# Decoder layer on one core: products of exponentials and values, four heads at a time in place of two

## The chip, the core and the metric

The kernel runs on one core of a Trainium2 chip. The metric is the device time of one execution in microseconds (us). Five engines work side by side: TensorE (PE, with its weight loads as PEld), VectorE (DVE), ScalarE (ACT), GpSimd (POOL) and SyncE (SP), which here issues all transfers.

## The reference

The layer takes x (32 sequences of 64 rows, 256 wide) and a context of the same shape. Each of three steps is followed by a residual sum and a normalization: causal self-attention with 16 heads of 16; a cross-attention with rotary positions; a two-matrix feed-forward part with quantized weights. The change touches the cross-attention only. It treats the 64 rows of a sequence as 64 channels (8 heads of 8 channels) and the 256 columns as positions:

```python
q = _apply_rotary(q_emb, split_heads(_proj(x, Wq, bq)))   # 8 heads, 256 positions, 8 channels
k = _apply_rotary(k_emb, split_heads(_proj(c, Wk, bk)))
v = split_heads(_proj(c, Wv, bv))
scores = jnp.einsum('bhtc,bhsc->bhts', q, k) / math.sqrt(K_CH)
p_attn = jax.nn.softmax(scores, axis=-1)
out = jnp.einsum('bhts,bhsc->bhtc', p_attn, v)
```

## The kernel before

**Tiling.** The 32 sequences are 16 pairs; a pair fills 128 partitions. The order of every engine's work is written out by hand. Phase A does both attentions for all pairs in a software pipeline of 16 bodies, one per pair `i`; most are in a hardware loop (`Fori`). Two more phases do the feed-forward part and aren't touched.

**A body has 16 slots.** In body i, slot s, TensorE does:

- `max_tile` (L541): scores of two heads, for the row maxima, 14 tiles ahead. From slot 2 on these are tiles of pair i+1.
- `exp_tile` (L561): the same scores, transposed and with the negated maximum added through two extra rows of `QA`, into bank `e_b[s % 2]`.
- one piece of other work of the pipeline, if the slot has one (below).
- `pv_tile` of the tile before, s - 1 (L576): exponentials times values.

ScalarE turns each `e_b` bank into exponentials, 128x512, in `PB[:, n % 4]` (L731), so four tiles fit. VectorE reduces each max tile (L912).

**pv_tile.** Tile n holds two heads and 128 of the 256 key positions. For each head one matmul contracts over the 128 positions: 32 stationary columns (8 channels, and ones whose product is the sum of the exponentials, up to the 32 of a column group) and 256 moving columns, float32, into PSUM partitions 32j to 32j+31. j is `2 * hp + e`, hence a tile uses two of the four 32-wide column groups; the next tile, with `hp = 1`, uses the other two. A float32 matmul shows as two records in the trace.

**Other work in the slots**, with j = i+2 and a = i+3: slot 0 `qk_proj(a)` (L454); 1 `u_transpose` (L226); 2 `max_transpose(i, 1)` (L549); 3 `transpose_p(j)` (L485); 4 `self_pv(j)` (L498: 16 matmuls of 32 stationary and 64 moving columns, float32, over the four column groups); 5 `out_proj(j)` (L507) and `att_transpose` (L233); 6 `rotary_proj("k", j)`; 7 `x_out_proj`; 8 `rotary_proj("q", j)`; 9 `xv_proj`; 11 `v_proj(a)`; 12 `u_transpose` and `max_transpose(i+1, 0)`; 13 and 14 `scores(a)` (L469, L473). Slots 10 and 15 have none.

**From a projection to the scores of a pair.** This is the longest detour of the pipeline. After `out_proj(j)` in slot 5, VectorE takes the statistics of the first normalization (L873 to L878), POOL the root (L292, L294), VectorE normalizes (L885) and rotates k and q (L893). POOL splits k and then q into three bfloat16 parts (`split_parts`, L835 to L845, five operations each). SP stores the parts of k in HBM (L331), issues the loads that spread them over `KA` (L345), stores the parts of q (L331), stores the row maxima (`max_rows`, L359, from `MR` into two rows of `QA`), moves `VM` (L354), waits until the parts of q have landed, and issues the three loads of `QA` (L345). SP does all this in this order. The next body's slot 2 begins with the max tile that reads this `QA` (pair j = i+2 of body i is the next pair of body i+1). The exp tile of slot 0 waits for the row maxima from `max_rows`.

Of the kernel before, what the change touches and what calls it, by code (L numbers as in the profile page):

```python
# [27 lines left out]
NPAIR = 16  # L28
# [42 lines left out]
def build_layer(nc, x, xT, ctx, wpT, woT, xW, xB, rows, w1T, w2T, attn_tables, rotary_tables, out):  # L71
    with ExitStack() as outer:
# [11 lines left out]
        def event(name, steps=1):  # L84
            return Event(sem(name), steps)
# [108 lines left out]
        mrow = [[sem(f"mrow{p}{b}") for b in range(2)] for p in range(2)]  # L194
        mx_ps, mx_red, negm = event("mx_ps", 16), event("mx_red", 16), event("negm", 4)
        mt_ps, mt_sb = event("mt_ps", 2), event("mt_sb", 2)
        e_ps, e_sb, pv = event("e_ps", 16), event("e_sb", 16), event("pv", 16)
        s_wabs, s_wtot, s_wq = sem("s_wabs"), sem("s_wtot"), sem("s_wq")
        s_wround, s_wclip = sem("s_wround"), [sem(f"s_wclip{k}") for k in range(2)]
        NEXPAND = 16 * 3  # L200
# [3 lines left out]
        def wait(eng, ev, pair, step):  # L204
            eng.wait_ge(ev.sem, ev.at(pair, step))  # L205
# [233 lines left out]
        def _(pe):  # L439
# [123 lines left out]
                                            QA[0:K_EXP, 2 * i.p + b, h, :], start=True, stop=True)  # L563
                last.then_inc(e_ps.sem, 1)

            def pv_tile(i, n):

                b, (s4, sc, hp) = n // 8, ((n // 4) % 2, (n // 2) % 2, n % 2)
                if n % 8 == 0:
                    wait(pe, xv_sb, i, 1)  # L570
                    if has(i, 1):
                        wait(pe, u_sb, i.plus(-1), b + 1)
                wait(pe, e_sb, i, n + 1)
                for e in range(2):
                    j = 2 * hp + e
                    last = nc.tensor.matmul(u_b[b][32 * j:32 * j + 32, D * s4:D * s4 + D],  # L576
                                            VA[:, i.p, sc, b, 4 * s4 + j, :], PB[:, n % 4, e, :],
                                            start=sc == 0, stop=sc == 1)
                last.then_inc(pv.sem, 1)

# [40 lines left out]
            def body(i, first=False, selfs=True, rotary=True, last=False):  # L621
# [9 lines left out]
                for s in range(16):  # L631
                    nxt, n = tile_at(i, s + AHEAD)
                    if not last or s + AHEAD < 16:
                        max_tile(nxt, n)
                    exp_tile(i, s)
                    if s == 0 and not first:
                        pv_tile(prev, 15)
                    if s == 0 and selfs:
                        qk_proj(a)
                    if s == 1 and not first:  # L640
                        u_transpose(pe, prev, 1, use(g_b[1], u_nrm, prev, 4))
                    if s == 2:
                        max_transpose(i, 1, 0)
                    if s == 3 and rotary:
                        transpose_p(j)
                    if s == 4 and rotary:
                        self_pv(j)
                    if s == 5 and rotary:
                        out_proj(j)
                    if s == 5 and not first:  # L650
                        att_transpose(pe, prev, use(g_b[1], at_sb, prev, 1))
                    if s == 7 and not first:
                        x_out_proj(pe, prev, use(g_b[0], ln2, prev, 1))
                    if s == 8 and rotary:
                        rotary_proj("q", g_b[1], j)
                    if s == 6 and rotary:
                        rotary_proj("k", g_b[1], j)
                    if s == 9 and not last:
                        xv_proj(i.plus(1))
                    if s == 11 and selfs:  # L660
                        v_proj(a)
                    if s == 12:
                        u_transpose(pe, i, 0, use(g_b[0], u_nrm, i, 2))
                        if not last:
                            max_transpose(i.plus(1), 0, 1)
                    if s == 13 and selfs:
                        scores(a, (0,))
                    if s == 13 and isinstance(i.v, int) and i.v == 13:
                        weight_total(1)
                    if s == 14 and selfs:  # L670
                        scores(a, (1,))
                    if s:
                        pv_tile(i, s - 1)

            bodies(pe, body)
            pv_tile(Pair(0, NPAIR - 1), 15)


        @block.scalar
        def _(act):  # L680
# [46 lines left out]
            def exp_tile(i, n):  # L727
                wait(act, e_ps, i, n + 1)
                if has(i, 1) or n >= 4:
                    act.wait_ge(pv.sem, 16 * i.v + n - 3)  # L730
                nc.scalar.activation(PB[:, n % 4].rearrange("p e t -> p (e t)"), e_b[n % 2][:, :], ACT.Exp,  # L731
                                     scale=XC ** -0.5).then_inc(e_sb.sem, 1)

            def u_copy(i, b):
                wait(act, pv, i, 8 * b + 8)
                if b == 1:
                    wait(act, ut_ps, i, 1)
                elif has(i, 1):
                    wait(act, ut_ps, i.plus(-1), 2)
                nc.scalar.activation(US[:].rearrange("p s t -> p (s t)"), u_b[b][:, :], ACT.Copy).then_inc(u_sb.sem, 1)  # L740
# [108 lines left out]
        def _(dve):  # L849
# [47 lines left out]
            def xv_bias(v):  # L897
                wait(dve, xv_ps, v, 1)
                if has(v, 2):
                    wait(dve, pv, v.plus(-2), 16)  # L900
                dst = VA[:, v.p].rearrange("p s b h c -> p (s b) h c")[:, :, :, 0:XC]
                nc.vector.tensor_tensor(
                    dst, g_b[0][:, 0:D].rearrange("p (q h c) -> p q h c", q=4, h=XH),
# [549 lines left out]
```

## Time and profile before

| | |
|---|---|
| time, median of 3 runs | 742.56 us (738.97 to 747.3) |
| span of the profiled execution | 750.5 us |
| PE busy | 583.4 us, 78% |
| DVE busy | 532.3 us, 71% |
| ACT busy | 387.6 us, 52% |
| POOL busy | 314.5 us, 42% |
| exponentials times values (L576) | 165.7 us busy, 1024 records |

The profiled execution's own time is its span; no other time of it is given. Phase A takes the first 570 us of it, the two feed-forward phases the rest. Busy time counts the union of the records of an engine, so matmuls that run side by side in different column groups count once. "Idle before" is how long an engine stood still ahead of an instruction, with what ended that. PEclk is TensorE's granted clock, 1.00 being 2.4 GHz and 0.50 being 1.2 GHz; a value between is a stretch with both.

### The profile page before, as it was taken

Reading aid. Unit: us, or ns where it says so; the run is one execution under the profiler, and the core shown is the slowest. Engines: PE = TensorE matmul, PEld = TensorE weight load, DVE = VectorE, ACT = ScalarE, POOL = GpSimd, SP = SyncE. Lnnn points to the kernel's source line nnn. Section 1 sums busy time; section 2 is a strip of 40 time slices with the busy share of each in tenths; the row PEclk is TensorE's granted clock in tenths of the full one; section 3 lists DMA queues with packets and bytes.
Section 4 is the critical chain, followed back from the end, with each engine's and each line's share of the span. In section 5 each row is a group of like instructions: output and inputs, shape, how many; then the busy total and the mean of one; then the engine's idle time right before and its main releaser. Section 6 shows DMA issues by size and latency. Waiting matters only on the chain. (4 is left out here: it accounts for less than half of the span.)

```text
span 750.5 us, 13775 instructions
## 1 busy us (share of the span) xinstructions
PE 583.4 (78%) x4002; PEld 319.4 (43%) x4002; DVE 532.3 (71%) x1081; ACT 387.6 (52%) x682; POOL 314.5 (42%) x382
## 2 busy tenths in 40 slices
PE   4656798998989989899998989988697632555455
PEld 3441445454554545445454454534242211333333
DVE  5468376867768777686877878757463767888886
ACT  3220344544545445444555444546565886777764
POOL 3432344443424544244452444514002006776764
PEclk9676699999999999999999999989897885555555
DMA  7112411212121121211212112121100000000000
GB/s 224 48 33 57 152 37 54 65 37 65 42 58 40 52 69 32 68 41 53 64 36 68 44 52 61 35 56 36 34 2 0 1 0 0 14 14 21 14 22 29
DMA packets 60044, 34.37 MB, mean 46 GB/s; under 512 B 20976, under 2 KB 59248, under 8 KB 59888
## 3 DMA queue, kind: packets, MB, share of 16 engines
q1 hardware_dynamic: 60016, 34.03, 15.3%
q8 instruction: 13, 0.21, 0.1%
q14 instruction: 15, 0.12, 0.1%
HBM read 24.32 MB, written 8.39 MB: 44 GB/s over the span
## 5 line engine op out<-in xcount | busy, mean ns | idle before, releaser
L731 ACT ACTIVATE PB<-e_b 128x512 f32<-128x512 f32 x256 | 152.5, 597 | 207.5 <-PE e_b L561 205.6
L912 DVE TENSOR_REDUCE MX<-mx_b 128x2 f32<-128x512 f32 x256 | 174.2, 686 | 100.2 <-PE mx_b L541 97.3
L576 PE MATMUL u_b<-PB,VA 128*32 128x256 f32 x1024 | 165.7, 403 | 0.8 <-ACT PB L731 0.6
L541 PE MATMUL mx_b<-KA,QA 96*128 96x256 bf16 x512 | 105.7, 291 | 35.7 <-DMA QA<-parts_q 32.2
L561 PE MATMUL e_b<-QA,KA 98*128 98x256 bf16 x512 | 102.5, 282 | 6.9 <-DMA QA<-MR 6.9
L541 PEld LDWEIGHTS mx_b<-KA,QA 96*128 96x128 bf16 x512 | 31.1, 99 | 140.8 <-issue 90.2
L827 POOL TENSOR_TENSOR SP<-SP,srec 128x1024 f32<-128x1024 f32 x14 | 26.6, 1901 | 129.1 <-DVE srec L868 129.1
L292 POOL TENSOR_TENSOR rs<-mv,epsc 128x1 f32<-128x1 f32 x32 | 7.0, 217 | 168.5 <-DVE mv L878 120.3
L576 PEld LDWEIGHTS u_b<-PB,VA 128*32 128x32 f32 x1024 | 37.9, 109 | 65.7 <-ACT PB L731 38.6
L1330 PE MATMUL r_b<-att_tab,Q 128*128 128x128 f32 x128 | 31.3, 426 | 37.5 <-ACT Q L1254 37.3
L822 POOL TENSOR_TENSOR KM<-QK,att_tab 128x1024 f32<-128x1024 f32 x30 | 56.5, 1904 | 7.2 <-ACT QK L686 7.2
L561 PEld LDWEIGHTS e_b<-QA,KA 98*128 98x128 bf16 x512 | 50.3, 102 | 21.4 <-DMA QA<-MR 8.0
L1322 PE MATMUL z_b<-w2q,Q2T 128*128 128x256 bf16 x128 | 29.3, 408 | 37.0 <-ACT Q2T L1277 26.3
L1330 PEld LDWEIGHTS r_b<-att_tab,Q 128*128 128x128 f32 x128 | 25.1, 223 | 45.1 <-ACT Q L1254 38.1
L1287 POOL TENSOR_TENSOR rsh<-mvh,epsc 128x1 f32<-128x1 f32 x16 | 15.2, 948 | 57.1 <-DVE mvh L1350 57.1
L1297 POOL TENSOR_TENSOR N<-N,row_tab 128x1024 f32<-128x1024 f32 x16 | 37.6, 2347 | 1.9 <-ACT N L1261 1.9
L1322 PEld LDWEIGHTS z_b<-w2q,Q2T 128*128 128x128 bf16 x128 | 16.3, 138 | 48.9 <-DVE stz L1368 24.9
L454 PE MATMUL g_b<-XT,wp 128*128 128x128 f32 x224 | 32.0, 302 | 5.5 <-DMA XT<-in_xT 5.5
L454 PEld LDWEIGHTS g_b<-XT,wp 128*128 128x128 f32 x224 | 29.4, 211 | 10.5 <-DMA wp<-in_wpT 5.5
L473 PE MATMUL g_b<-KM,QK 128*64 128x512 f32 x112 | 30.2, 618 | 0.0
L854 DVE TENSOR_REDUCE smax<-g_b 128x8 f32<-128x512 f32 x28 | 19.4, 692 | 14.0 <-PE g_b L473 14.0
L1254 ACT ACTIVATE Q<-N,rnd,sc 128x1024 f32<-128x1024 f32 x16 | 19.9, 1241 | 17.6 <-DVE sc L1380 9.9
(201 smaller groups left out, 1131.7 us busy)
## 6 DMA issues: line engine op xcount, KB each, us to landing
KA<-parts_k SPq DMA_DIRECT2D x96, 64.0 KB
QA<-parts_q SPq DMA_DIRECT2D x96, 64.0 KB
parts_k<-part_k SPq DMA_DIRECT2D x16, 192.0 KB, 1.9
parts_q<-part_q SPq DMA_DIRECT2D x16, 192.0 KB, 5.1
XT<-in_xT SPq DMA_DIRECT2D x16, 128.0 KB, 5.3
X<-in_x SPq DMA_DIRECT2D x16, 128.0 KB, 4.1
C<-in_ctx SPq DMA_DIRECT2D x16, 128.0 KB, 4.0
out_y<-O SPq DMA_DIRECT2D x16, 128.0 KB, 1.7
```

The source lines that it names most:

```text
L454: last = nc.tensor.matmul(ps[:, P * c:P * c + P], wp[:, k, P * c:P * c + P], XT[:, a.p, k, :], start=k == 0, stop=k == 1)
L473: last = nc.tensor.matmul(ps[SEQ * b:SEQ * b + SEQ, :], QK[:, c, SEQ * b:SEQ * b + SEQ], KM[:, c, :, SEQ * b:SEQ * b + SEQ], start=False, ...
L541: last = nc.tensor.matmul(mx_b[n % 2][:, D * e:D * e + D], QA[0:K_MAX, 2 * i.p + b, h, P * u:P * u + P], KA[0:K_MAX, 2 * i.p + b, h, :], s ...
L561: last = nc.tensor.matmul(e_b[n % 2][:, D * e:D * e + D], KA[0:K_EXP, 2 * i.p + b, h, P * sc:P * sc + P], QA[0:K_EXP, 2 * i.p + b, h, :], ...
L576: last = nc.tensor.matmul(u_b[b][32 * j:32 * j + 32, D * s4:D * s4 + D], VA[:, i.p, sc, b, 4 * s4 + j, :], PB[:, n % 4, e, :], start=sc == ...
L731: nc.scalar.activation(PB[:, n % 4].rearrange("p e t -> p (e t)"), e_b[n % 2][:, :], ACT.Exp, scale=XC ** -0.5).then_inc(e_sb.sem, 1)
L822: ops.tensor_tensor(KM[:, c], QK[:, 2 + c, :].unsqueeze(1).broadcast_to([P, 8, P]), kmask.unsqueeze(2).broadcast_to([P, 8, P]), ALU.mult). ...
L827: ops.tensor_tensor(SP[:], SP[:], srec[:].unsqueeze(2).broadcast_to([P, SH, SEQ]), ALU.mult).then_inc(s_norm.sem, 1)
L912: nc.vector.tensor_reduce(MX[:, b, 2 * hp:2 * hp + 2, u], mx_b[n % 2][:, :].rearrange("p (e s) -> p e s", e=2), AXL.X, ALU.max).then_inc(m ...
L1297: nc.gpsimd.tensor_tensor(N[:, k.p, :], N[:, k.p, :], gam, ALU.mult).then_inc(zg.sem, 1)
L1322: m = nc.tensor.matmul(z_b[j.p][:, 0:D], Q2T[:, j.p, k, :], w2q[:, k, :], start=k == 0, stop=k == 7)
L1330: t = nc.tensor.transpose(r_b[j.p][:, P * k:P * k + P], Q2[:, j.p, P * k:P * k + P], ident)
```

## The change

`pv_tile(i, n)` becomes `pv_quad(i, m)`. It takes the tiles 2m and 2m+1 together: four matmuls, one in each column group, after a wait for the later of the two tiles. It stands in the even slots (quad s/2 - 1 in slot s) and, for the last quad of a pair, in slot 0 of the next body. The semaphore `pv` counts 8 steps a pair in place of 16, and the waits on it are rewritten to match.

```diff
-            def pv_tile(i, n):
-                b, (s4, sc, hp) = n // 8, ((n // 4) % 2, (n // 2) % 2, n % 2)
-                if n % 8 == 0:
+            def pv_quad(i, m):
+                b, s4, sc = m // 4, (m // 2) % 2, m % 2
+                if m % 4 == 0:
                     wait(pe, xv_sb, i, 1)
                     if has(i, 1):
                         wait(pe, u_sb, i.plus(-1), b + 1)
-                wait(pe, e_sb, i, n + 1)
-                for e in range(2):
-                    j = 2 * hp + e
+                wait(pe, e_sb, i, 2 * m + 2)
+                for j in range(4):
                     last = nc.tensor.matmul(u_b[b][32 * j:32 * j + 32, D * s4:D * s4 + D],
-                                            VA[:, i.p, sc, b, 4 * s4 + j, :], PB[:, n % 4, e, :],
+                                            VA[:, i.p, sc, b, 4 * s4 + j, :], PB[:, (2 * m + j // 2) % 4, j % 2, :],
                                             start=sc == 0, stop=sc == 1)
                 last.then_inc(pv.sem, 1)
...
                     if s == 0 and not first:
-                        pv_tile(prev, 15)
+                        pv_quad(prev, 7)
...
-                    if s:
-                        pv_tile(i, s - 1)
+                    if s and s % 2 == 0:
+                        pv_quad(i, s // 2 - 1)
...
             def exp_tile(i, n):
                 wait(act, e_ps, i, n + 1)
                 if has(i, 1) or n >= 4:
-                    act.wait_ge(pv.sem, 16 * i.v + n - 3)
+                    act.wait_ge(pv.sem, 8 * i.v + n // 2 - 1)
...
             def u_copy(i, b):
-                wait(act, pv, i, 8 * b + 8)
+                wait(act, pv, i, 4 * b + 4)
```

The first place is TensorE in the loop, from slot 2's `max_transpose` (L549) to the products of slot 3, behind the transposes of slot 3 (L485). "ISA" and "REGISTER_ALU" rows compute and set up waits. Before:

```order
L549 MATMUL g_b0<-identb,NM 32x128
L205 REGISTER_ALU
L576 MATMUL u_b0<-PB,VA 32x256 x2
L541 MATMUL mx_b1<-KA,QA 128x256 x2
L561 MATMUL e_b1<-QA,KA 128x256 x2
L205 REGISTER_ALU
L444 ISA
L485 MATMUL g_b1<-att_tab,SP 128x128 x4
L444 ISA
L485 MATMUL g_b0<-att_tab,SP 128x128 x4
L205 REGISTER_ALU
L576 MATMUL u_b0<-PB,VA 32x256 x2
```

The change, the same place:

```order
L549 MATMUL g_b0<-identb,NM 32x128
L205 REGISTER_ALU x2
L575 MATMUL u_b0<-PB,VA 32x256 x4
L541 MATMUL mx_b1<-KA,QA 128x256 x2
L561 MATMUL e_b1<-QA,KA 128x256 x2
L205 REGISTER_ALU
L444 ISA
L485 MATMUL g_b1<-att_tab,SP 128x128 x4
L444 ISA
L485 MATMUL g_b0<-att_tab,SP 128x128 x4
L538 REGISTER_ALU
L541 MATMUL mx_b0<-KA,QA 128x256 x2
```

The group of slot 2 has four matmuls in place of two (the line is now L575), and slot 3's is gone: the max tile of slot 4 comes right behind the transposes.

The second place is TensorE at the turn of a body, from the products of slot 0 over `qk_proj` (L454) and slot 1 to its end. Before:

```order
L576 MATMUL u_b1<-PB,VA 32x256 x2
L450 ISA
L444 ISA
L454 MATMUL g_b0<-XT,wp 128x128 x8
L538 REGISTER_ALU
L541 MATMUL mx_b1<-KA,QA 128x256 x2
L561 MATMUL e_b1<-QA,KA 128x256 x2
L444 REGISTER_ALU
L205 ISA
L226 MATMUL g_b1<-att_tab,US 128x128 x4
L205 REGISTER_ALU x3
L576 MATMUL u_b0<-PB,VA 32x256 x2
```

The change:

```order
L575 MATMUL u_b1<-PB,VA 32x256 x4
L450 ISA
L444 ISA
L454 MATMUL g_b0<-XT,wp 128x128 x8
L538 REGISTER_ALU
L541 MATMUL mx_b1<-KA,QA 128x256 x2
L561 MATMUL e_b1<-QA,KA 128x256 x2
L444 REGISTER_ALU
L205 ISA
L226 MATMUL g_b1<-att_tab,US 128x128 x4
L535 ISA
L538 ISA
```

Slot 0 has the four products of the last pair's quad, and slot 1 has none: the max tile of slot 2 comes right behind `u_transpose` (L226). On SP, DVE, ACT and POOL no operation is added, removed or moved.

## Rows read from the trace of the kernel before

**Rows 1.** the page: TensorE busy; its granted clock in 40 slices:

```profile
PE 583.4 (78%) x4002; PEld 319.4 (43%) x4002; DVE 532.3 (71%) x1081; ACT 387.6 (52%) x682; POOL 314.5 (42%) x382
...
PEclk9676699999999999999999999989897885555555
```

**Rows 2.** waits, PE, 111 to 500 us: us in total, times, longest:

```profile
PE mx_b L541 <- DMA QA<-parts_q: 27.0, 13, 2.9
```

**Rows 3.** timeline, PE, slots 0 to 2: start, us, instruction, idle before it:

```profile
305.32 0.38 PE L561 MATMUL e_b<-QA,KA 98*128 98x256 bf16 x2
...
309.05 0.63 PE L576 MATMUL u_b<-PB,VA 128*32 128x256 f32 x4
311.59 0.39 PE L541 MATMUL mx_b<-KA,QA 96*128 96x256 bf16 x2 [1.92 <-DMA QA<-parts_q]
```

**Rows 4.** timeline, DVE, first normalization of the pair:

```profile
287.14 0.42 DVE L873 TENSOR_TENSOR Y<-g_b,X 128x256 f32<-128x256 f32 x1 [0.49 <-PE g_b L507]
```

**Rows 5.** timeline, POOL, splits of k and of q:

```profile
290.60 0.73 POOL L835 TENSOR_TENSOR full_k<-rot_k 128x256 f32<-128x256 f32 x1 [1.40 <-DVE rot_k L893]
...
297.99 0.67 POOL L845 TENSOR_TENSOR part_q<-full_q,part_q 128x256 bf16<-128x256 f32 x1
```

**Rows 6.** timeline, SP, issues behind the split of q:

```profile
298.75 1.49 SPq L331 DMA_DIRECT2D parts_q<-part_q  x1
300.37 0.63 SPq L359 DMA_DIRECT2D QA<-MR  x1
...
304.03 2.44 SPq L345 DMA_DIRECT2D QA<-parts_q  x3
```

**Rows 7.** timeline, PE, slots 2 to 5 of another body, at full clock:

```profile
248.84 0.62 PE L576 MATMUL u_b<-PB,VA 128*32 128x256 f32 x4
249.39 0.39 PE L541 MATMUL mx_b<-KA,QA 96*128 96x256 bf16 x2
...
249.84 1.04 PE L485 MATMUL g_b<-att_tab,SP 128*128 128x128 f32 x8
...
251.91 0.69 PE L498 MATMUL g_b<-PT,VM 128*32 128x64 f32 x32
252.43 0.61 PE L576 MATMUL u_b<-PB,VA 128*32 128x256 f32 x4
...
253.42 1.03 PE L507 MATMUL g_b<-wout,AO 128*128 128x256 f32 x4
254.28 0.38 PE L233 MATMUL g_b<-att_tab,AN 128*128 128x128 f32 x2
```

**Rows 8.** timeline, ACT, slot 3 of that body:

```profile
250.04 0.60 ACT L731 ACTIVATE PB<-e_b 128x512 f32<-128x512 f32 x1 [0.28 <-PE e_b L561]
250.54 1.08 ACT L711 ACTIVATE PT<-g_b 128x512 f32<-128x512 f32 x2
```

**Rows 9.** restart to out_proj: us, PE busy, PEclk, DMA share, GB/s:

```profile
118.63:126.35 7.72, 7.72 (x75) 0.78 0.13 38
248.29:254.45 6.16, 6.16 (x75) 1.00 0.15 42
468.33:474.48 6.15, 6.15 (x75) 1.00 0.15 43
498.95:507.66 8.71, 8.71 (x75) 0.68 0.15 44
```

**Rows 10.** timeline, PE, the turn of bodies 13 and 14:

```profile
526.12 0.39 PE L561 MATMUL e_b<-QA,KA 98*128 98x256 bf16 x2 [2.55 <-DMA QA<-MR]
...
534.18 0.61 PE L541 MATMUL mx_b<-KA,QA 96*128 96x256 bf16 x2 [5.14 <-DMA QA<-parts_q]
```

**Rows 11.** timeline, SP, the row maxima of that turn:

```profile
522.18 0.63 SPq L359 DMA_DIRECT2D QA<-MR  x1
```

**Rows 12.** timeline, PE, body 15:

```profile
557.57 0.63 PE L576 MATMUL u_b<-PB,VA 128*32 128x256 f32 x4
...
558.45 0.63 PE L576 MATMUL u_b<-PB,VA 128*32 128x256 f32 x4
```

More of the change, by code:

```diff
@@ L196, in build_layer @@
         mt_ps, mt_sb = event("mt_ps", 2), event("mt_sb", 2)
-        e_ps, e_sb, pv = event("e_ps", 16), event("e_sb", 16), event("pv", 16)
+        e_ps, e_sb, pv = event("e_ps", 16), event("e_sb", 16), event("pv", 8)
         s_wabs, s_wtot, s_wq = sem("s_wabs"), sem("s_wtot"), sem("s_wq")
@@ L671, in body @@
                         scores(a, (1,))
-                    if s:
-                        pv_tile(i, s - 1)
+                    if s and s % 2 == 0:
+                        pv_quad(i, s // 2 - 1)
             bodies(pe, body)
-            pv_tile(Pair(0, NPAIR - 1), 15)
+            pv_quad(Pair(0, NPAIR - 1), 7)
         @block.scalar
@@ L899, in xv_bias @@
                 if has(v, 2):
-                    wait(dve, pv, v.plus(-2), 16)
+                    wait(dve, pv, v.plus(-2), 8)
                 dst = VA[:, v.p].rearrange("p s b h c -> p (s b) h c")[:, :, :, 0:XC]
```

## Prediction

> **What bounds the kernel now.** I read the page first, then the waits of TensorE, then the timelines of PE, DVE, POOL and SP over one body, then a table of stretches. On the page [rows 1] the reader sees TensorE busy for 78% of the span and its clock near full through phase A: this looks like a TensorE-bound phase, in which fewer or shorter products must pay. The waits say something else. From 111 to 500 us TensorE has in effect one wait, for the three loads of QA, 13 times, 27.0 us in all, 2.1 us each [rows 2]. It comes in slot 2 of every body, ahead of the first max tile of the next pair [rows 3].
>
> So the question is what sets that landing. I follow it back. `out_proj` of the pair ends in slot 5 of the body before, and VectorE takes its statistics at 287.14 us [rows 4]. POOL starts on k at 290.60 and is done with q at 298.66 (297.99 + 0.67), ten split operations and a root without a pause [rows 5]. SP stores q at 298.75, waits for that store, issues the loads of QA at 304.03 [rows 6], and TensorE goes on at 311.59 [rows 3]. None of these steps waits for a product of exponentials and values. From the end of `out_proj` at about 286.9 to 311.59 it is 24.7 us, and it is nearly the same in other bodies: 474.48 to 498.95 [rows 9] is 24.5. The rest of the period is the stretch from the restart in slot 2 to the end of `out_proj` in slot 5: 6.15 us at full clock, 7.7 with part of it at half clock, 8.7 with most of it at half clock [rows 9]. The period is the sum: a loop of latency (24.6) and a short stretch (S) of TensorE. Only what changes S changes the time of the loop. **A product saved in slots 5 to 1 lengthens the wait in slot 2.**
>
> **Step 1, the price of a quad.** A tile's two products take 0.55 us from start to the next start (248.84 to 249.39) [rows 7], where one float32 product of 256 columns at full width takes 0.43 (`out_proj`: two in 254.28 - 253.42 = 0.86) [rows 7]. So two column groups already run side by side. Do four? `self_pv` does exactly this: 16 products of 64 columns over four groups, as many columns as a quad, in 252.43 - 251.91 = 0.52 [rows 7]. The bounds are 0.52 and, if only two ran together, 1.10. I take 0.57, the pair's 0.55 and a little for two more starts, since `self_pv` is nearest in shape. By the Trainium skill (TensorEngine Tiling (Array Packing), Key Properties) a change of tiling mode drains TensorE, which would give fewer drains with quads; the rows show the same as 0.55 against 0.43, and that is in my price.
>
> **Step 2, what leaves the path that doesn't set the end.** From behind `out_proj` to slot 2 there are 13 tiles' products (slots 5 to 15, 0, 1) and there will be 6 quads: 13 x 0.55 - 6 x 0.57 = 3.7 us less work a body. All of it turns into waiting, because QA lands when it did. It will be in two places. The exp tile of slot 0 (now 305.32 [rows 3]) would come 11 x 0.55 - 5 x 0.57 = 3.2 us earlier, at 302.1; but it needs the row maxima, which SP issues at 300.37, behind the store of q [rows 6]. At the turn to body 14 they were issued at 522.18 [rows 11] and TensorE went on at 526.12 [rows 10], 3.9 us later; so here at 304.3. That is a new wait of some 2 us in slot 0. The rest, 1.9 + 3.7 - 2.2 = 3.4 us, is the wait in slot 2.
>
> **Step 3, S at full clock.** Slots 2, 3 and 4 issue three tiles' products before `out_proj`, and will issue two quads: 3 x 0.55 - 2 x 0.57 = 0.5 less. But the tile's products of slot 3 cover the two copies on ScalarE that `self_pv` needs; these end at 250.54 + 1.08 = 251.62 [rows 8]. With the cover gone `self_pv` can start at about 251.67 and not at 251.91 - 0.55 = 251.36. So 0.3 comes back as a wait, and S becomes 6.16 - 0.2 = 5.95.
>
> **Step 4, the clock in S.** Between 118 and 475 us there are 12 restarts, from the first to the third row of [rows 9]. Without the longest, the waits average (27.0 - 2.9) / 12 = 2.0 us [rows 2]. Seven S are 7.64 to 7.72 with a mean clock of 0.78, five are 6.15 or 6.16 at 1.00. Mean 7.05. After a wait of 2.9 us S was 8.71 [rows 9]; after the one of 5.14 us the first max tile takes 0.61 us [rows 10] where it takes 0.39 at full clock [rows 3]. Longer waits go with more time at half clock. With 3.4 us in slot 2 and 2 us just before, I expect hardly any full-clock S: 7.7 less 0.3 is 7.4, 8.71 less 0.55 (at half clock slot 3's products cost more, and ScalarE covers less) is 8.15. I take 7.6, between them. That is 0.55 us more a body, **12 x 0.55 = +6.6 us**. Bodies 0 and 13 restart at half clock already and gain 0.55 each: -1.1. The Trainium skill (TensorE: Matmul & The Clock Gate, "What's actually happening") says that the throttled clock is the default and activity releases it. By that every S would be of the 8.15 kind, +13.2 in place of +6.6; the five full-clock restarts show that a wait of 2 us does not always do it, and no row shows what two waits close together do.
>
> **Step 5, the tail.** Bodies 14 and 15 have no such loop behind them. The first half of body 14 waits for transfers (5.14 us [rows 10], and then row maxima). In its second half a quad saves 2 x 0.55 - 0.57 = 0.53, less some 0.25 of a new wait: nothing stands any more between an exp tile and the quad that needs its exponentials but one max and one exp tile. Four quads: -1.1. Body 15 runs at 0.88 a slot [rows 12]. With quads the round is exponentials (0.60 [rows 8]), quad (0.57), exp tile (0.38 [rows 3]) and handing over between engines, some 1.65 for two slots in place of 1.76, seven times: -0.8. ScalarE and the semaphore leave no more. The feed-forward phases aren't touched. Tail: -1.9.
>
> **Sum.** +6.6 - 1.1 - 1.9 = +3.6 us on the profiled execution, 750.5 to 754. That execution lies 7.9 us above the median of 742.56. The three runs differ by 8.3 us, and between no slow S and seven lie 7 x 1.55 = 10.9 us; so the median run may well have had fewer slow S, and then the change costs it more than 3.6. If it had two, the mean S was 6.4 and the loss 12 x 1.2 - 3.0 = +11.4. I take 742.6 + 3.6 and some 2 for this: **748 us**. About 1% (735.1 to 750.0) is what a measurement of this kernel can tell from no change.
>
> **Rivals.**
>
> *The clock falls for long at every restart, and the change is slower* (0.18). Place: slots 2 and 3. Price: S 8.15 in all 12 bodies against a mean of 6.4 to 7.05, +13.2 to +21, less 3.0: 753 to 760. It decides as soon as waits of 3 us always leave half clock behind. For it speaks the row of 8.71; against it that the slot-0 wait may slow slots 0 and 1 instead, fill the wait with slow work and let TensorE come to slot 2 warm.
>
> *The clock holds* (0.14). If two waits bring no more half clock, or if slow work fills them, S is near 5.95 in all bodies: 12 x (5.95 - 7.05) - 3.0 = -16.2, some 727.
>
> *TensorE was the bound after all* (0.03). If the landing of QA moved forward with TensorE, each body would save 16 x 0.55 - 8 x 0.57 = 4.2, or 60 us: 683. Against it stand the 13 waits and the fixed 24.6 us.
>
> *The groups don't run four at a time, or nothing shifts* (0.15). A quad at 1.10 leaves TensorE's work as it is; S then changes by 2 x 1.10 - 3 x 0.55 = +0.55 less the cover, the clock as before: 742 to 748.
>
> **Chances.** The forecast has 0.50: 0.02 of it under 735.1, 0.32 within 1%, 0.16 above 750. Faster: 0.14 + 0.03 + 0.02 = 0.19. Same: 0.32 + 0.12 = 0.44. Slower: 0.16 + 0.18 + 0.03 = 0.37. The range leaves out most of the two fast cases and the far end of the slow one: 735 to 757.
>
> **What the profile after would show.** Step 1: the products' busy time falls from 165.7 to 128 x 0.65, some 83 us. Step 2: a wait for the row maxima in slot 0 of each body, about 2 us, and one for QA in slot 2 of over 3 us; from the end of `out_proj` to the restart still 24.6. Step 3: `self_pv` waits 0.3 for ScalarE's copies. Step 4: a mean clock below 0.78 in most S, mean S 7.4 to 8.15. It is wrong if the 24.6 us shrink (a step of the detour that I took as fixed waits for TensorE), or if S is mostly at 1.00.

## The result: slower by 3.3%

The change takes 767.86 us (median of four runs, 763.33 to 773.39) against 743.0 us (four runs, 738.97 to 747.3) before: a ratio of 1.0332, with a 95% interval of 1.0259 to 1.0405. The profiled execution has a span of 764.8 us, 14.3 us over that of before. The forecast was 748 us, the range 735 to 757: the time lies outside it, on the side of the slower rival and beyond it. Every ratio here leaves out runs that took over 1.5% more than the fastest of their kernel (none in this comparison; of before, 9 of 19, 9 of 18 and 2 of 13 in the three sets of runs behind the experiments), so a ratio can differ from the quotient of two medians over all runs.

The page and the waits of TensorE in the loop:

```profile
PE 553.5 (72%) x4002; PEld 336.5 (44%) x4002; DVE 533.6 (70%) x1081; ACT 391.3 (51%) x682; POOL 314.8 (41%) x382
...
PEclk9676799887979898899998879988698795555555
```

```profile
PE mx_b L541 <- DMA QA<-parts_q: 27.3, 12, 3.7
PE e_b L561 <- DMA QA<-MR: 19.6, 11, 2.2
PE g_b L549 <- DVE NM L924: 10.2, 10, 1.4
```

TensorE is busy for 30 us less than in [rows 1], and its waits in the loop have gone from 27 us to 57. The wait for QA is as in [rows 2]. The wait for the row maxima is new, as forecast in step 2. The third is new too, and no step of the prediction has it: `max_transpose` (L549) waits for NM, the negated maxima that VectorE makes. One turn of a body shows how the three hang together. TensorE:

```profile
244.57 0.39 PE L561 MATMUL e_b<-QA,KA 98*128 98x256 bf16 x2 [2.04 <-DMA QA<-MR]
244.89 0.64 PE L575 MATMUL u_b<-PB,VA 128*32 128x256 f32 x8
245.46 3.55 PE L454 MATMUL g_b<-XT,wp 128*128 128x128 f32 x16
248.80 0.57 PE L541 MATMUL mx_b<-KA,QA 96*128 96x256 bf16 x2
...
251.78 0.39 PE L541 MATMUL mx_b<-KA,QA 96*128 96x256 bf16 x2 [1.75 <-DMA QA<-parts_q]
...
253.70 0.29 PE L549 MATMUL g_b<-identb,NM 128*32 128x128 bf16 x1 [1.31 <-DVE NM L924]
253.88 1.08 PE L575 MATMUL u_b<-PB,VA 128*32 128x256 f32 x8
...
255.72 1.91 PE L485 MATMUL g_b<-att_tab,SP 128*128 128x128 f32 x8
...
258.49 1.07 PE L498 MATMUL g_b<-PT,VM 128*32 128x64 f32 x32
...
260.38 1.03 PE L507 MATMUL g_b<-wout,AO 128*128 128x256 f32 x4
```

The exp tile of slot 0 waits 2.04 us for the row maxima. Behind it `qk_proj` (L454) takes 3.55 us; it takes 2.05 in every body from 1 to 12 of before. The granted clock during `qk_proj`, here and in a body of before (us, PE busy, PEclk, DMA share, GB/s), says why:

```profile
245.46:248.80 3.34, 3.34 (x21) 0.54 0.11 31
```

```profile
306.19:308.07 1.88, 1.88 (x18) 1.00 0.13 40
```

A clock of 0.54 is nearly all 1.2 GHz, 1.00 is 2.4 GHz.

Then come the wait for QA (1.75), the restart at 251.78, and 1.31 us for NM. The quads and all that follows run late and partly at half clock. GpSimd, ScalarE and VectorE in the same stretch:

```profile
245.61 1.90 POOL L826 TENSOR_TENSOR SP<-SP,srec 128x1024 f32<-128x1024 f32 x1 [6.76 <-DVE srec L867]
249.87 3.75 POOL L821 TENSOR_TENSOR KM<-QK,att_tab 128x1024 f32<-128x1024 f32 x2 [2.36 <-ACT QK L685]
```

```profile
249.19 0.60 ACT L685 ACTIVATE QK<-g_b 128x512 f32<-128x512 f32 x1 [2.92 <-PE g_b L454]
```

```profile
249.40 0.69 DVE L911 TENSOR_REDUCE MX<-mx_b 128x2 f32<-128x512 f32 x1 [3.88 <-PE mx_b L541]
250.23 1.56 DVE L922 TENSOR_SCALAR NM<-MX 128x16 bf16<-128x16 f32 x1
251.83 1.82 DVE L924 SCALAR_TENSOR_TENSOR NM<-MX,NM 128x16 bf16<-128x16 f32 x1
```

ScalarE copies QK only at 249.19, because `qk_proj` is late. `k_mask` on GpSimd needs this copy and starts at 249.87: two operations (L821) until 253.62. VectorE's two operations for NM, 128x16 each, are ready just then. L922 takes 1.56 us, L924 1.82; each takes 0.17 where it runs undisturbed. The first ends at 251.79, half way through `k_mask`, the second at 253.65, with its end. In the kernel before the same place looks like this:

```profile
309.32 0.50 DVE L923 TENSOR_SCALAR NM<-MX 128x16 bf16<-128x16 f32 x1
309.85 1.82 DVE L925 SCALAR_TENSOR_TENSOR NM<-MX,NM 128x16 bf16<-128x16 f32 x1
```

```profile
309.74 3.75 POOL L822 TENSOR_TENSOR KM<-QK,att_tab 128x1024 f32<-128x1024 f32 x2
```

```profile
312.13 0.23 PE L549 MATMUL g_b<-identb,NM 128*32 128x128 bf16 x1
```

There VectorE came to NM at 309.32, ahead of `k_mask` (309.74 to 313.49): it waited out the end of the operation before, then one operation of `k_mask`, and was done at 311.67. TensorE restarted at 311.59 and came to `max_transpose` at 312.13, so NM was ready with 0.46 us to spare. Now it comes to NM at 250.23, behind the start of `k_mask`, and waits out both. It is late because its input, the max tile of slot 1 (248.80), stands behind `qk_proj` too.

The stretch S (restart in slot 2 to the end of `out_proj`), with the columns of [rows 9]:

```profile
217.98:227.18 9.20, 8.32 (x79) 0.63 0.15 42
251.78:261.41 9.63, 8.31 (x79) 0.65 0.15 42
353.85:361.09 7.24, 7.23 (x79) 0.76 0.15 42
```

Ten of the twelve bodies have S of 8.53 to 9.63 us and a wait for NM of 0.70 to 1.40 us. The two others (the third row is one) have no such wait and S of 7.24 and 7.33; in them `qk_proj` took 2.05 us. The ledger of the profiled executions, worked out from the ends of `out_proj` and the restarts:

| part | forecast | measured |
|---|---|---|
| latency from `out_proj` to the restart, mean of 12 | 24.6, unchanged | 24.65 before, 24.64 after |
| S, mean of 12 | 7.05 to 7.6 | 7.05 to 8.87, **+21.8 us in the 12 bodies** |
| bodies 0 and 13 | -1.1 | -1.8 - 1.4 = -3.2 |
| behind the last `out_proj` | -1.9 | 242.8 to 238.6 = -4.2 |
| sum | +3.6 | +14.4 |

### The profile page after: what moved, and what is told of

It is laid out like the page before. It is cut to its first block and busy times, and to the rows that moved or that the text cites. A ratio compares the mean times of both kernels' runs of the same rounds, so it can differ in the third digit from the quotient of the medians.

```text
span 764.8 us, 13769 instructions
## 1 busy us (share of the span) xinstructions
PE 553.5 (72%) x4002; PEld 336.5 (44%) x4002; DVE 533.6 (70%) x1081; ACT 391.3 (51%) x682; POOL 314.8 (41%) x382
## 5 line engine op out<-in xcount | busy, mean ns | idle before, releaser
L911 DVE TENSOR_REDUCE MX<-mx_b 128x2 f32<-128x512 f32 x256 | 171.0, 681 | 121.4 <-PE mx_b L541 120.7
L541 PE MATMUL mx_b<-KA,QA 96*128 96x256 bf16 x512 | 110.2, 301 | 39.0 <-DMA QA<-parts_q 34.7
L561 PE MATMUL e_b<-QA,KA 98*128 98x256 bf16 x512 | 107.6, 296 | 31.5 <-DMA QA<-MR 30.6
L575 PE MATMUL u_b<-PB,VA 128*32 128x256 f32 x1024 | 90.5, 425 | 4.0 <-ACT PB L730 3.8
L541 PEld LDWEIGHTS mx_b<-KA,QA 96*128 96x128 bf16 x512 | 39.9, 104 | 118.1 <-issue 59.7
L561 PEld LDWEIGHTS e_b<-QA,KA 98*128 98x128 bf16 x512 | 52.3, 106 | 49.2 <-DMA QA<-MR 22.0
L821 POOL TENSOR_TENSOR KM<-QK,att_tab 128x1024 f32<-128x1024 f32 x30 | 56.4, 1900 | 29.1 <-ACT QK L685 29.1
L454 PE MATMUL g_b<-XT,wp 128*128 128x128 f32 x224 | 45.5, 386 | 5.6 <-DMA XT<-in_xT 5.6
L454 PEld LDWEIGHTS g_b<-XT,wp 128*128 128x128 f32 x224 | 42.1, 289 | 11.4 <-issue 5.7
L1321 PEld LDWEIGHTS z_b<-w2q,Q2T 128*128 128x128 bf16 x128 | 16.6, 140 | 49.4 <-DVE stz L1367 24.9
L575 PEld LDWEIGHTS u_b<-PB,VA 128*32 128x32 f32 x1024 | 23.0, 115 | 34.6 <-ACT PB L730 21.8
L485 PE MATMUL g_b<-att_tab,SP 128*128 128x128 f32 x120 | 28.1, 414 | 5.0 <-DVE SP L826 5.0
```

The lines of the kernel that those rows point to most:

```text
L454: last = nc.tensor.matmul(ps[:, P * c:P * c + P], wp[:, k, P * c:P * c + P], XT[:, a.p, k, :], start=k == 0, stop=k == 1)
L541: last = nc.tensor.matmul(mx_b[n % 2][:, D * e:D * e + D], QA[0:K_MAX, 2 * i.p + b, h, P * u:P * u + P], KA[0:K_MAX, 2 * i.p + b, h, :], s ...
L561: last = nc.tensor.matmul(e_b[n % 2][:, D * e:D * e + D], KA[0:K_EXP, 2 * i.p + b, h, P * sc:P * sc + P], QA[0:K_EXP, 2 * i.p + b, h, :], ...
L821: ops.tensor_tensor(KM[:, c], QK[:, 2 + c, :].unsqueeze(1).broadcast_to([P, 8, P]), kmask.unsqueeze(2).broadcast_to([P, 8, P]), ALU.mult). ...
L911: nc.vector.tensor_reduce(MX[:, b, 2 * hp:2 * hp + 2, u], mx_b[n % 2][:, :].rearrange("p (e s) -> p e s", e=2), AXL.X, ALU.max).then_inc(m ...
L1321: m = nc.tensor.matmul(z_b[j.p][:, 0:D], Q2T[:, j.p, k, :], w2q[:, k, :], start=k == 0, stop=k == 7)
```

## The experiments

**Theory A:** the work that the quads save outside S turns into idling in slot 0; this brings half clock, `qk_proj` comes late, and with it `k_mask` and VectorE's last max tile; VectorE can't make NM beside `k_mask`, and `max_transpose` makes TensorE wait behind the restart. **Theory B:** S is long only because TensorE restarts at half clock after longer idling; the wait for NM costs nothing of its own. **Theory C:** the loss is the missing work, and returns when work is put back. **Rival D:** the place of the quads in the slots costs the time, whatever TensorE does between.

For every kernel the table gives the median, the ratio to the runs of before on the same chip with its interval, and from the profiled execution: the time from the end of `out_proj` in body 0 to that in body 12, the mean S of these bodies, and how many of them have a wait of over 0.5 us for NM. The medians of before over all runs beside them were 743.0 (the change), 746.3 (e1, e2, e3, e5), 750.8 (e4, e6, e7, e8) and 746.9 (e9, e10, e12), so ratios compare kernels better than times. The last three columns are of one execution each, which needn't be a middle one: for e1, e3 and e8 it was the fastest, and the profile of before (750.5 us) lies above its four runs.

| kernel | us | ratio | 12 bodies | S | waits for NM |
|---|---|---|---|---|---|
| before | 743.0 | | 380.4 | 7.05 | 0 |
| the change | 767.86 | 1.033 (1.026 to 1.041) | 402.2 | 8.87 | 10 |
| e1 change, k_mask held | 747.98 | 1.007 (1.004 to 1.011) | 384.1 | 7.36 | 0 |
| e2 change, row maxima first | 759.97 | 1.020 (1.012 to 1.029) | 394.4 | 8.03 | 0 |
| e10 change, filler in slot 0 | 755.83 | 1.014 (1.008 to 1.020) | 389.4 | 7.93 | 0 |
| e3 change, work put back | 754.16 | 1.018 (1.013 to 1.024) | 379.2 | 7.03 | 0 |
| e5 change, filler in slot 2 | 735.58 | 0.986 (0.979 to 0.994) | 371.7 | 6.3 | 2 |
| e6 change, both mendings | 733.27 | 0.988 (0.981 to 0.996) | 369.7 | 6.2 | 0 |
| e8 quads outside S | 750.73 | 1.015 (1.004 to 1.025) | 379.3 | 6.9 | 3 |
| e7 quads inside S | 744.49 | 1.001 (0.997 to 1.005) | 373.9 | 6.55 | 0 |
| e9 before, k_mask held | 741.0 | 0.989 (0.985 to 0.994) | 371.6 | 6.28 | 0 |
| e4 before, filler in slot 2 | 734.25 | 0.988 (0.982 to 0.993) | 369.5 | 6.15 | 0 |
| e12 combined | 730.1 | 0.980 (0.974 to 0.986) | 369.9 | 6.15 | 0 |

In e4, e5, e6, e8 and e12 some restarts left no idle time to find them by; there the restart is the first max tile of slot 2 by the order of the instructions.

### e1: k_mask held back

```diff
                 if selfs:
+                    wait(pool, negm, i, 4)
                     k_mask(pool, nc.gpsimd, a)
```

> The change, with GpSimd's k_mask (two operations of 1.9 us) held back until VectorE has made the negated maxima NM of the pair. Theory A (the new wait of max_transpose in slot 2 comes from k_mask, which now starts late and runs while VectorE makes NM, so that two operations of 0.17 us take 1.6 and 1.8): NM takes 0.17 us each, max_transpose never waits, the stretch S from the restart in slot 2 to the end of out_proj falls from 8.87 us on average to that of the two bodies without this wait, 7.3, and the run is 12 x 1.5 = 18 us faster than the change, about 749. Theory B (S is long only because TensorE runs at half clock after longer idling; the wait for NM is covered): the wait vanishes, but S stays above 8.5 and the time within 4 us of the change, 764 to 768.

747.98 us, against 767.86 for the change. VectorE and GpSimd in a body with a wait of 1.82 us in slot 0 and `qk_proj` at 3.33 us:

```profile
237.47 0.17 DVE L922 TENSOR_SCALAR NM<-MX 128x16 bf16<-128x16 f32 x1
237.68 0.17 DVE L924 SCALAR_TENSOR_TENSOR NM<-MX,NM 128x16 bf16<-128x16 f32 x1
```

```profile
238.08 3.75 POOL L821 TENSOR_TENSOR KM<-QK,att_tab 128x1024 f32<-128x1024 f32 x2 [3.07 <-DVE NM L924]
```

```profile
231.85 0.39 PE L561 MATMUL e_b<-QA,KA 98*128 98x256 bf16 x2 [1.82 <-DMA QA<-MR]
...
233.06 3.33 PE L454 MATMUL g_b<-XT,wp 128*128 128x128 f32 x16
...
238.85 0.39 PE L541 MATMUL mx_b<-KA,QA 96*128 96x256 bf16 x2 [1.58 <-DMA QA<-parts_q]
...
239.40 0.23 PE L549 MATMUL g_b<-identb,NM 128*32 128x128 bf16 x1
...
242.44 0.68 PE L498 MATMUL g_b<-PT,VM 128*32 128x64 f32 x31 [0.53 <-ACT PT L710]
```

NM takes 0.17 us twice, `k_mask` starts behind it, and `max_transpose` follows the restart (238.85) at 239.40 without a wait. That is all this edit does, and it gives back 20 us of medians: theory B, which expected 764 or more, falls as it was stated. Not all 20 are the loop's: body 0, which waited 3.08 us for NM, ends 6.2 us earlier by the profiles, and this it does in the kernel before too (e9). The 12 bodies are 18.1 us shorter, but in the fastest of ten executions (742.52); in a middle one it must be less. The last row also shows step 3: `self_pv` now waits 0.53 us for ScalarE's copies at full clock.

### e2 and e10: two ways to get k_mask early

e2 stores the row maxima ahead of the parts of q; e10 lets TensorE work where it waits in slot 0.

```diff
                     store_parts("k", i.plus(2))
                     expand_rows("k", i.plus(2), 0)
-                    store_parts("q", i.plus(2))
                 if not last:
                     max_rows(i.plus(1), 0)
+                if rotary:
+                    store_parts("q", i.plus(2))
```

> The change, with SyncE storing the row maxima of the next pair before it stores the parts of q. Theory A (the wait in slot 0 for the row maxima slows the clock there, qk_proj then takes 3.5 us in place of 1.9, and k_mask starts late): the wait in slot 0 goes, qk_proj is at full clock, k_mask is done in time, the wait for QA in slot 2 grows to about 5.5 us, max_transpose doesn't wait, S falls to about 7.4 and the time to about 750. Against it: the store of q is issued some 0.7 us later if the row maxima are not there yet, 8 us over the loop. Theory B (long idling alone makes S long): a wait of 5.5 us in one piece leaves S at 8.5 or more, time 764 or above.

```diff
                     nxt, n = tile_at(i, s + AHEAD)
+                    if s == 0 and not first:
+                        pe.wait_ge(mx_red.sem, 16 * i.v + 13)
+                        for _ in range(7):
+                            nc.tensor.matmul(mx_b[0][:, :], QA[0:K_MAX, 2 * i.p + 1, 0, 0:P],
+                                             KA[0:K_MAX, 2 * i.p + 1, 0:2, :], start=True, stop=True)
```

> The change, with seven products of 512 columns in bf16 (1.5 us at full clock, results overwritten) at the head of slot 0, where TensorE waits for the row maxima; nothing in slot 2, k_mask not held. Theory A (the wait in slot 0 brings half clock, so qk_proj is late, so k_mask is late, so NM is late): qk_proj takes 1.9 us again in most bodies, no wait for NM, S about 7.4, time 748 to 753, as with k_mask held (748.0). If k_mask is late for another reason, the wait for NM stays and the time is 762 or more.

In e2 slot 0 still waits 1.0 to 1.6 us, but `qk_proj` is at 2.05 in nine of the 12 bodies and NM is never waited for by more than 0.2 us in the loop. That the slot-0 wait stays, and the time of 760 between the 750 of theory A and the 764 of B, were not expected, so e2 settles little by itself. In e10 it is 2.05 in all twelve. TensorE in one body of e10:

```profile
237.94 1.67 PE L635 MATMUL mx_b<-KA,QA 96*128 96x512 bf16 x7
...
240.23 0.39 PE L561 MATMUL e_b<-QA,KA 98*128 98x256 bf16 x2 [0.40 <-DMA QA<-MR]
...
241.12 2.05 PE L454 MATMUL g_b<-XT,wp 128*128 128x128 f32 x16
...
247.19 0.39 PE L541 MATMUL mx_b<-KA,QA 96*128 96x256 bf16 x2 [3.14 <-DMA QA<-parts_q]
...
247.87 0.29 PE L549 MATMUL g_b<-identb,NM 128*32 128x128 bf16 x1
248.05 1.08 PE L575 MATMUL u_b<-PB,VA 128*32 128x256 f32 x8
```

The filler stands where TensorE waited, the rest of that wait is 0.40 us, `qk_proj` takes 2.05, and `max_transpose` comes 0.68 us after the restart, where it came 1.92 after it in the change. No body of the loop waits for NM. This is theory A's middle link: nothing touched `k_mask` or VectorE, only the idling and the clock ahead of `qk_proj`. But the time saved is idled in slot 2 instead, 3.14 us here, and the last row shows the quad at 1.08 us, half clock. S is 7.57 to 8.28 in all twelve bodies of e10 and the time, 755.8, lies 3 us above what I had expected: part of theory B holds beside A. Long idling without a late NM costs about a microsecond a body (7.93 and 8.03 against 7.05).

### e3: work put back

```diff
+                    if s in (1, 5, 7, 9, 11, 13, 15) and not last:
+                        if has(nxt, 1) or n >= 2:
+                            pe.wait_ge(mx_red.sem, 16 * nxt.v + n - 1)
+                        for _ in range(5):
+                            nc.tensor.matmul(mx_b[n % 2][:, 0:D], QA[0:K_MAX, 2 * i.p + 1, 0, 0:P],
+                                             KA[0:K_MAX, 2 * i.p + 1, 0, :], start=True, stop=True)
```

> The change, with five products of 256 columns in bf16 ahead of the max tile in seven slots (5 to 15 and 1, odd ones): work of 0.53 us each whose results are overwritten, 3.7 us a body, as much as the quads took away there. Theory C (the loss is the work that was taken away outside slots 2 to 5: it turned into idling, and this costs clock and the late k_mask): slot 0 no longer waits for the row maxima, the wait in slot 2 is about 2 us, S is 6 to 7.5 us and the time is back to that of the kernel before or a little under it, 738 to 747. Rival D (the place of the quads in the slots costs the time, whatever TensorE does in between): S stays above 8.5 and the time at 760 or more.

```profile
PE mx_b L541 <- DMA QA<-parts_q: 26.6, 13, 3.4
PE g_b L498 <- ACT PT L716: 4.5, 9, 0.5
```

The two largest waits are that of the kernel before and the one for ScalarE's copies; the row maxima and NM are waited for once each, 0.5 and 0.4 us. The loop takes 379.2 us, S is 7.03: theory C holds for the loop of this execution, and rival D (S above 8.5, 760 us or more) falls. The median, though, is 754.2 us, 12 us above the forecast's middle and outside its range, and the ratio of 1.018 leaves about half of the loss in place. The profiled execution was the fastest of ten (747.42), so this profile doesn't show where the others lose; that stays open.

### e5, e4 and e6: work in place of idling in slot 2

e5 and e4 differ in the kernel (the change, before) and the count (10, 8); e6 is e5 with the edit of e1.

```diff
+                    if s == 2 and not last:
+                        pe.wait_ge(mx_red.sem, 16 * nxt.v - 1)
+                        for _ in range(10):
+                            nc.tensor.matmul(mx_b[0][:, :], QA[0:K_MAX, 2 * i.p + 1, 0, 0:P],
+                                             KA[0:K_MAX, 2 * i.p + 1, 0:2, :], start=True, stop=True)
```

> The change, with ten products of 512 columns in bf16 at the head of slot 2, where TensorE waits for QA: 2.1 us at full clock, 4.3 at half clock; their results are overwritten. Theory B (the idling in slot 2 is what slows S): the clock is up at the restart in most bodies, S falls to between 6.5 and 7.5 even with a wait for NM, and the time to 735 to 750. Theory A (k_mask is late because of the wait in slot 0): the wait for NM of about 1 us stays, S is 7.5 to 8 at full clock, and the time about 752.

> The kernel before, with eight products of 512 columns in bf16 at the head of slot 2 (1.7 us at full clock), whose results are overwritten. The kernel before idles there for 2 us a body, and 7 of 12 stretches S were partly at half clock, 1.55 us longer each. If the clock after the idling is worth this, all S become 6.15 us, the latency from out_proj to the landing of QA stays 24.6, and the run is about 11 us faster than the profiled run of before: 733 to 740. If the quads are what makes the warmed change fast, this kernel stays at 743.

> The change with both mendings: k_mask held back until NM is made, and ten products of 512 columns at the head of slot 2. If the late k_mask and the clock are the two costs and nothing else is, S is 6.1 in nearly all bodies, body 0 is 3 to 4 us shorter (it too waits for NM, 1.6 us in the warmed change), and the time is 2 to 4 us under that of the warmed change alone (735.6): about 732. If the warmed change had already removed both, it stays at 735.

Stretches S of e5, and TensorE's waits in the loop of e4:

```profile
180.81:186.93 6.12, 5.60 (x79) 1.00 0.14 42
333.58:339.67 6.09, 5.59 (x79) 1.00 0.14 42
```

```profile
PE mx_b L541 <- DMA QA<-parts_q: 2.4, 4, 1.1
```

With a filler in slot 2 every S of e4 is 6.14 to 6.16, those of e5 from body 3 on are 6.09 to 6.40 with the clock at 1.00, and both kernels have the same time (734.3 and 735.6). Useless products make either kernel 1.2 to 1.4% faster than before. The time of e5 is in the range that theory B had given (735 to 750) and not at theory A's 752. NM is waited for in bodies 1 and 2 (0.78 and 1.12 us) and then no more, against what theory A had expected: once S is short and the clock up, the wait in slot 0 is split (from body 3 on 0.6 to 1.0 us of it moves to slot 8, where the other row maxima are awaited), `qk_proj` stays at 2.05 and NM is in time. In the change no body of the loop waits in slot 8, and slot 0 waits 1.4 us or more in one piece. So the late NM seems to feed itself: a long S lets slot 8 pass without waiting, and all idling then falls in slot 0. This fits the rows of both kernels; no run tests it by itself. e6 takes 2 us less than e5 by medians (the wait for NM in body 0 is gone), though not by ratios, and its 12 bodies take 369.7 us, those of e4 369.5: with both mendings the quads cost nothing in the loop any more.

### e7, e8 and e8 again: which quads do it

Both are the kernel before with quads for some of the tiles.

```diff
+            def products(i, n):
+                if n // 2 not in (0, 1):       # e7; e8: (2, 3, 4, 5, 6, 7)
+                    pv_tile(i, n)
+                elif n % 2:
+                    pv_quad(i, n // 2)
...
-                        pv_tile(i, s - 1)
+                        products(i, s - 1)
```

> The kernel before with quads for the tiles 0 to 3 alone (slots 2 and 4; slots 1 and 3 have no products), all other tiles two heads at a time as before. It takes 0.55 us of work away ahead of the wait in slot 2. Theory A: slot 0 stays on time (no wait for the row maxima), k_mask is on time, S is as in the kernel before or 0.2 us less, the time within 5 us of before, 738 to 747. Rival D (the place of the quads in slots 2 to 5 makes S long): S above 8, time above 755.

> The kernel before with quads for the tiles 4 to 15 alone; the tiles 0 to 3 two heads at a time in slots 1 to 4. It takes 3.2 us of work away before slot 0 and none in slots 2 to 5. Theory A: as in the change, a wait of about 1.7 us in slot 0, qk_proj at half clock, a wait of about 1 us for NM in most bodies, S 9 to 9.5 us, time 760 to 775 although nothing in slots 2 to 5 is changed. Rival D: S as in the kernel before, 7.05, time 740 to 747.

> The same kernel as e8_quads_outside_S (quads for the tiles 4 to 15 alone), whose profile was of its fastest execution (742.66 us) while its median was 750.73. A second look at another execution. If the late NM is a matter of how the wait in slot 0 falls in each body, a slower execution shows more bodies with qk_proj over 3 us and a wait for NM (3 of 13 in the first), each with S of 7.2 us or more: at 751 us some 6 to 8 of 13. If the difference lies in the latency or in the feed-forward phases, their number stays at 3.

With quads in slots 2 to 5 alone (e7) nothing is lost: ratio 1.001, no slot-0 wait, no wait for NM; nine of its S are 6.08 to 6.18. Where nothing in slots 2 to 5 is changed (e8) the ratio is 1.015 (1.004 to 1.025), but the median of 750.7 is that of before over all runs on the same chip (750.8): a loss isn't clearly shown, and theory A's 760 to 775 with S of 9 to 9.5 is missed. S is 6.9, near what rival D had for this kernel. The wait in slot 0 is there in all bodies, but in the first profile, of its fastest execution (742.66), it starves `qk_proj` of the clock in only three. In the second profile (746.93) there are four; here is one of them:

```profile
361.71 0.39 PE L561 MATMUL e_b<-QA,KA 98*128 98x256 bf16 x2 [1.81 <-DMA QA<-MR]
...
362.62 3.62 PE L454 MATMUL g_b<-XT,wp 128*128 128x128 f32 x16
...
369.01 0.39 PE L541 MATMUL mx_b<-KA,QA 96*128 96x256 bf16 x2 [1.34 <-DMA QA<-parts_q]
...
370.93 0.23 PE L549 MATMUL g_b<-identb,NM 128*32 128x128 bf16 x1 [1.31 <-DVE NM L945]
```

A wait of 1.81 us in one piece, `qk_proj` at 3.62, and 1.31 us for NM in slot 2, although slots 2 to 5 are those of the kernel before. The number of such bodies fell short of the six to eight that I had expected. So the chain can start outside S, as theory A has it, and rival D, by which the quads in slots 2 to 5 make S long, falls by e7. But neither half of the quads brings the loss of the change: it takes both. Why the chain catches hold in 3 or 4 bodies here and in 10 of 12 in the change isn't shown; the feeding back described under e5 would explain it.

### e9: the same hold in the kernel before

> The kernel before with k_mask held back until NM is made. In it NM is waited for in body 0 alone (3.06 us). If the late k_mask is a cost of the change and not of the kernel before, the loop is as before and only body 0 gains: 2 to 4 us less than before, a ratio of 0.995 to 1.0.

741.0 us, ratio 0.989 (0.985 to 0.994), more than I had expected. The edit is that of e1. Body 0 no longer waits for NM (3.06 us in the profile of before), its S is 6.2 us in place of 11.8, and it ends 7.2 us earlier, which is more than the 5.9 us of the medians. The loop of this profile has S at 6.15 in 11 of 12 bodies, which the edit doesn't explain, since NM wasn't waited for there. Runs of before differ by as much among themselves. This run also puts e1 in its place: with `k_mask` held in both kernels the change is still slower, by 0.9% (747.98 against 741.0) or, by the two ratios, 1.8%. So the late NM makes up some half to three quarters of the 3.3%. The rest goes in the loop when TensorE is kept at work in slot 2 (e4 and e6).

### e12: combined

```diff
+            def products(i, n):
+                if not (isinstance(i.v, int) and i.v >= 14):
+                    pv_tile(i, n)
+                elif n % 2:
+                    pv_quad(i, n // 2)
```

with the hold of e1 and the filler of e4.

> A version put together from what the runs showed: two heads at a time in bodies 0 to 13, quads in bodies 14 and 15 alone (behind the loop the change was 4.2 us faster from the end of the last out_proj to the end of the span: 238.6 against 242.8), k_mask held, eight products of 512 columns at the head of slot 2. If the parts add up: the warmed kernel before (734.3) less 4 for the tail and less 1.4 for body 0, 728 to 731. If the tail's gain came from elsewhere, 733 to 734.

730.1 us (729.83 to 732.0), ratio 0.980 (0.974 to 0.986): the fastest of all, 38 us under the change. From the last `out_proj` to the end of the span it is 238.9 us, where e4 takes 241.2: the tail's gain is the quads' in bodies 14 and 15. Of the other profiles those of the change, e1, e2, e3, e5, e6 and e10, with such quads, have 238.4 to 240.6, and those of before and e9, without them, 242.8 and 242.9. The tail in the change, body 15:

```profile
578.41 0.64 PE L575 MATMUL u_b<-PB,VA 128*32 128x256 f32 x8 [0.75 <-ACT PB L730]
...
580.06 0.64 PE L575 MATMUL u_b<-PB,VA 128*32 128x256 f32 x8
```

## Why the prediction was wrong, by its steps

**What bounds the kernel** was right. The latency from `out_proj` to the restart is on average 24.6 us in every kernel that ran, within 0.3, and only S moved the loop.

**Step 1, the quad at 0.57,** was right: 244.89 to 245.46. The four groups do run side by side, and the rival with a quad at 1.10 falls. The products' busy time is 90.5 us, 83 having been forecast, since more of them run at half clock.

**Step 2, the saved work becomes two waits,** was right in place, and in size for slot 0: 1.4 to 2.2 us there (2.2 forecast). In slot 2 it is 1.75 to 2.1 in ten bodies and 3.5 and 3.7 in the two without a late NM, where 3.4 was forecast. In the ten TensorE fills the difference with `qk_proj` at half clock, some 1.5 us longer, and the first max tile of slot 2 then still runs at full clock (251.78, 0.39 us). I had named slow work in slots 0 and 1 only as something that would shorten the second wait and help. I didn't ask who waits for `qk_proj`.

**Step 3, self_pv waits for ScalarE's copies,** was right in kind. At full clock the wait is 0.5 and not 0.3, and S is 6.09 to 6.12 in place of 5.95 (e1, e5, e7): the quads in S win next to nothing.

**Step 4 is the one that failed.** It made S a matter of the clock alone, 7.6 with 8.15 as the worst. The clock's part was about right: without the late NM, S is 7.36 (e1, in its fastest execution) to 8.03 (e2), where the forecast had 7.4 to 8.15. What it left out is the wait for NM: the late `qk_proj`, behind it `k_mask` (through ScalarE's copy) and VectorE's last max tile, VectorE's two small operations beside `k_mask`, `max_transpose` in slot 2. In the change that wait is 0.85 us a body on average by itself, and it keeps TensorE idle and at half clock longer: with it S is 8.87, with NM made first 7.36. 12 x 1.5 = 18 us of the 21.8 that the loop lost; e1 takes away 18.1. These are profiles, e1's of a fast execution; by medians and ratios the share is some half to three quarters (e9). The traces of before held both signs. Its DVE timeline has L925 at 1.82 us beside `k_mask` in slot 1, done 0.46 us before `max_transpose` needs it, so NM had little slack left. And its body 0 has the whole chain once, behind a wait of 4.33 us in slot 0:

```profile
77.70 3.62 PE L454 MATMUL g_b<-XT,wp 128*128 128x128 f32 x16
...
85.96 0.27 PE L549 MATMUL g_b<-identb,NM 128*32 128x128 bf16 x1 [3.06 <-DVE NM L925]
```

I had looked at neither as something that a later `qk_proj` would push. The prediction counts body 0 among those that "restart at half clock already"; its first max tile of slot 2 ran at full clock (82.28, 0.39 us), and what made its S long began with this wait for NM.

**Step 5, the tail,** had the pace right (1.65 us for two slots in body 15, as forecast) and the sum too small by 2.3 us.

**The median.** The remark that the median run of before may have had fewer slow S than its profile fits, though no profile of such a run was taken: the profiles differ by 14.3 us, the medians by 24.9. I had allowed 2 us for that and it was 10.6.

The slower rival, at 753 to 760, came nearest, with the wrong mechanism: its clock alone gives 7.9 to 8.0 (e10, e2), 756 to 760 us, and the late NM brings the rest.

## What to carry to other kernels

In a loop held by a latency, work saved outside the one stretch that TensorE paces comes back as idling, and the question is then where this idling falls, what the clock does to the instruction behind it, and which other engine's work that instruction releases. Look in the trace of before for small operations that take ten times their usual time: here they marked two engines that stood in each other's way, and a shift of some microseconds put them on the path. Where a fixed wait can't be shortened, filling it with throw-away products so that TensorE restarts at full clock was worth more here (1.2% less time) than taking 75 us from the busy time of its products (3.3% more).

## What the runs showed of the hardware

- **Two small operations of VectorE stand still beside GpSimd's.** Those for NM take 0.17 us each alone and 1.56 and 1.82 us beside `k_mask`; the second ends 0.03 us behind it (253.65 against 253.62). The Trainium skill (SBUF — State Buffer, "Who interferes with whom") says that VectorE contends with GpSimd for a shared port pair, which one of them holds for its whole instruction, when VectorE's operation has two SBUF inputs and GpSimd's reads SBUF, or when VectorE's runs in a two-port mode. The trace agrees: whole instructions of 1.9 us are waited out, and ordering the two engines (e1) ends it. The second operation (L924) has two SBUF inputs; the first has one, and whether it ran in a two-port mode no row shows. An operation with an input in PSUM wasn't held: L265 takes 0.29 us beside `k_mask` (311.87 in before) and 0.29 behind it (253.85 in the change).
- **Four column groups run as fast as two.** Eight records of a quad take 0.57 us from start to start, four of a pair of heads 0.55 [rows 7].
- **The clock after short idling isn't settled by the idling's length alone.** In the kernel before, waits of 1.66 to 2.5 us led to S of 6.15 in five bodies and 7.6 to 7.7 in seven; the granted clock between was 1.00 in the one kind and 0.78 in the other [rows 9]. With a filler it was 1.00. The Trainium skill (TensorE: Matmul & The Clock Gate, "What's actually happening") has the clock fall by default and rise with activity; the fillers, whose results nobody reads, bear this out.
